# Moving one rounding step of a weight quantization from VectorE to ScalarE, and two small loads to the head of a queue

## What is computed

```python
def _L0_attn_ref(x, w_qkv, w_proj):
    qkv = (x @ w_qkv.T).reshape(B, N, 3, H, hd)
    att = softmax(einsum('bnid,bnjd->bnij', q, k) * scale)
    out = einsum('bnij,bnjd->bnid', att, v)
    return out.transpose(0, 2, 1, 3).reshape(B, N, D) @ w_proj.T
def fake_quant(x, bits, axes):
    qmax = 2.0 ** (bits - 1) - 1.0
    amax = jnp.max(jnp.abs(x), axis=axes, keepdims=True)
    scale = jnp.where(amax > 0, amax / qmax, jnp.ones_like(amax))
    return jnp.clip(jnp.round(x / scale), -qmax, qmax) * scale
def _L0_ffn_ref(x, kernel, bias):
    y = relu(fake_quant(x) @ fake_quant(kernel, 8, 0) + fake_quant(bias))
    return fake_quant(y)
x = x + _L0_attn_ref(_layernorm(x), w_qkv, w_proj)
x = x + _L0_ffn_ref(_layernorm(x), kernel, bias)
```

## Time and profile before

| what | value |
|---|---|
| median of 2 timed runs | 986.57 us (985.31 to 987.83) |
| the profiled execution's own time | 912.17 us |
| span of the slowest core (6) in it; the 8 cores | 910.6 us; 896.6 to 910.6 us |
| busy: PE, DVE, ACT, POOL | 690.0 (76%), 566.2 (62%), 323.1 (35%), 110.9 (12%) us |
| mean granted TensorE clock | 0.864 to 0.870 of full |

### The profile page before, as it was taken

One profiled execution on the slowest core, in us unless ns is written; L12 is line 12 of the kernel. 1 busy time (PEld: TensorE's weight loads), 2 busy tenths in 40 slices (PEclk: granted clock), 3 DMA queues, 4 the chain that ended last, 5 costly groups with the idle time before them and its releaser, 6 DMA issues.

```text
span 910.6 us, 10967 instructions; the slowest of 8 cores (896.6 to 910.6 us)
## 1 busy us (share of the span) xinstructions
PE 690.0 (76%) x3524; PEld 340.9 (37%) x3584; DVE 566.2 (62%) x949; ACT 323.1 (35%) x363; POOL 110.9 (12%) x93
## 2 busy tenths in 40 slices
PE   1147999899999999995565669954976647978790
PEld 1023444344444444443444434520433323434340
DVE  3353335535554554435777738981688895999996
ACT  3366334324333433434555521210221324433320
POOL 1001111112111211100000000012000000123214
PEclk9998999999999999996555569985897967989996
DMA  9552989989999999846532264379322200111112
GB/s 159 140 169 39 83 81 145 149 121 151 157 148 152 158 150 105 79 47 200 135 44 39 36 190 125 116 145 177 86 67 80 93 0 1 47 47 47 74 65 92
DMA packets 116984, 94.20 MB, mean 103 GB/s; under 512 B 101184, under 2 KB 101312, under 8 KB 113856
## 3 DMA queue, kind: packets, MB, share of 16 engines
q0 software_dynamic: 103680, 33.56, 38.0%
q1 hardware_dynamic: 13248, 59.94, 19.2%
HBM read 118.65 MB, written 8.39 MB: 140 GB/s over the span
## 4 chain that ended last, share of the span: by engine, by line
DVE 27%; issue 10%; PE 7%; DMA 6%; ACT 3%; DVEq 1%; POOLq 0%; POOL 0%; ACTq 0%; SPq 0%
DMA wpb<-wpT 4%; DMA ktb<-wkT 2%; DVE bnbuf L591 2%; DVE cols L656 2%; DVE ktb L688 2%; DVE kti L692 2%; DVE ttile L799 2%; DVE xr L557 2%; PE pF L538 2%; DVE cols L802 2%; ACT Ebuf L358 1%; DVE cols L389 1%; DVE Abuf L398 1%; ACT aTTbuf L366 1%; PE pF L344 1%
## 5 line engine op out<-in xcount | busy, mean ns | idle before, releaser
L289 PE MATMUL pF<-aT,wqb 128*128 128x512 bf16 x736 | 280.0, 380 | 1.6
L287 PE MATMUL pF<-aT,wqb 128*128 128x512 bf16 x706 | 268.5, 380 | 4.4 <-ACT qT L114 3.0
L538 PE MATMUL pF<-qk,xqs 128*128 128x512 bf16 x500 | 117.1, 394 | 4.6 <-ACT xqs L885 3.7
L502 PE MATMUL pF<-wpb,sT 128*128 128x512 bf16 x240 | 99.4, 414 | 24.7 <-DMA wpb<-wpT 23.1
L505 PE MATMUL pF<-wpb,sT 128*128 128x512 bf16 x256 | 106.2, 415 | 4.0 <-DMA wpb<-wpT 1.8
L287 PEld LDWEIGHTS pF<-aT,wqb 128*128 128x128 bf16 x736 | 72.2, 98 | 92.9 <-issue 6.9
L289 PEld LDWEIGHTS pF<-aT,wqb 128*128 128x128 bf16 x736 | 72.2, 98 | 87.1 <-issue 1.1
L302 POOL DMA_DIRECT2D wqb<-wqkvT x48 | 55.1, 1148 | 338.5 <-PE pF L289 248.3
L113 DVE CAST qT<-pF 128x512 bf16<-128x512 f32 x16 | 42.9, 2682 | 70.3 <-PE pF L289 55.9
L113 DVE CAST vT<-pF 128x512 bf16<-128x512 f32 x16 | 42.6, 2662 | 58.8 <-PE pF L289 58.8
L538 PEld LDWEIGHTS pF<-qk,xqs 128*128 128x128 bf16 x512 | 51.6, 101 | 67.5 <-issue 12.9
(11 more groups left out here) (116 smaller groups left out, 843.7 us busy)
## 6 DMA issues: line engine op xcount, KB each, us to landing
wqb<-wqkvT POOLq DMA_DIRECT2D x48, 512.0 KB, 10.4
ktc<-wkT SPq DMA_DIRECT2D x32, 512.0 KB, 8.6
ktb<-wkT SPq DMA_DIRECT2D x32, 512.0 KB, 4.0
xbuf<-x_att SPq DMA_DIRECT2D x8, 1024.0 KB, 6.8
xr<-x_res SPq DMA_DIRECT2D x8, 1024.0 KB, 7.5
wpb<-wpT POOLq DMA_DIRECT2D x32, 256.0 KB, 6.2
out<-xr SPq DMA_DIRECT2D x7, 1024.0 KB, 3.8
bias_b<-bias SPq DMA_DIRECT2D x1, 1024.0 KB, 4.6
```

What stands on the lines that cost most here:

```text
L287: tn.matmul(pa[:, :], wch, aT[:, 1024 * c:1024 * c + 512], start=st, stop=sp)
L289: mm = tn.matmul(pb[:, :], wch, aT[:, 1024 * c + 512:1024 * c + 1024], start=st, stop=sp)
L502: tn.matmul(pF[2 * (idx % 2)][:, :], lhs, wpb[:, 1024 * m:1024 * m + 512], start=st, stop=sp)
L538: mm = tn.matmul(pF[u][:, :], xqs[Mt % 2][:, 128 * c:128 * (c + 1)], qk[:, 2048 * c + 512 * u:2048 * c + 512 * (u + 1)], start=(c == 0), s ...
```

## The change

The subtraction of MAGIC (before L692, VectorE) becomes an activation on ScalarE (Identity with a bias column that holds -MAGIC, written once by a memset), in front of the copies of the same step. Two semaphores are used in a new way: `fKb` (VectorE has multiplied and added) and `fKv` (now: ScalarE has subtracted). `_sLnexp` moves two steps later. The loads of `ident` and the mask move in front of those of x.

```diff
@@ stage 1, SyncE
+            inc(sync.dma_start(ident[:, :], d_ident[:, :]), "aCn", 16)
+            inc(sync.dma_start(mask4[:, :], d_mask[:, :]), "aCn", 16)
             for t in range(NT):
-                if t == 2:
-                    inc(sync.dma_start(ident[:, :], d_ident[:, :]), "aCn", 16)
-                    inc(sync.dma_start(mask4[:, :], d_mask[:, :]), "aCn", 16)
                 if t >= 2:
@@ projection, VectorE
+            inc(v.memset(col(12), -MAGIC), "gNM")
             for i in range(2 * NC):
@@
-                h_qb = inc(v.tensor_scalar(ktb[i % 2][:, :], ktb[i % 2][:, :],
-                                           cols[:, 64 + ft:65 + ft], MAGIC,
-                                           ALU.mult, ALU.add), "selfV")
-                wt(v, h_qb)
-                h_kv = inc(v.tensor_scalar(kti[i % 2][:, :], ktb[i % 2][:, :],
-                                           MAGIC, None, ALU.subtract), "fKv")
+                inc(v.tensor_scalar(ktb[i % 2][:, :], ktb[i % 2][:, :],
+                                    cols[:, 64 + ft:65 + ft], MAGIC,
+                                    ALU.mult, ALU.add), "fKb")
                 if i >= 3:
                     v.wait_ge(S_("fFt"), 2 * i - 4)
-                wt(v, h_kv)
+                v.wait_ge(S_("fKv"), i + 1)
                 inc(v.tensor_scalar_mul(kqb[i % 3][:, :], kti[i % 2][:, :],
                                         cols[:, 48 + ft:49 + ft]), "fKg")
@@ projection, ScalarE
+            s.wait_ge(S_("gNM"), 1)
             for fidx in range(2 * NC):
                 ft, hh = fidx // 2, fidx % 2
+                s.wait_ge(S_("fKb"), fidx + 1)
+                if fidx >= 2:
+                    s.wait_ge(S_("fKg"), fidx - 1)
+                inc(s.activation(kti[fidx % 2][:, :], ktb[fidx % 2][:, :],
+                                 AF.Identity, bias=col(12)), "fKv")
                 for b2 in range(2):
@@
-                if fidx % 2 == 0 and 18 <= fidx <= 28:
-                    _sLnexp(s, (fidx - 18) // 2)
+                if fidx % 2 == 0 and 20 <= fidx <= 30:
+                    _sLnexp(s, (fidx - 20) // 2)
```

## The result

| | before | changed |
|---|---|---|
| median | 912.02 us (10 runs) | 970.12 us (11 runs) |
| ratio to before | | 1.0654, 95% interval 1.0633 to 1.0676 |
| the profiled execution's own time | 912.17 us | 968.65 us |
| spans of the 8 cores | 896.6 to 910.6 us | 953.6 to 967.1 us |

The change costs 6.5%. Four of the ten executions before (984.11 to 987.83 us) and four of the eleven after (996.45 to 1047.85 us) are slow ones, with a lower granted clock on some cores wherever the cores are on record; the medians contain them, the ratio leaves them out, and both executions behind the 986.57 us that stood before the prediction are among them.

What follows compares the result with a forecast made beforehand. In the projection stage PE was taken to bound the first half and DVE the second. Stage terms summing to 61.4 us, with 0.8 for the loads, made 62, added to the 986.57 us median: 1049 us, range 1022 to 1075.

Steps and rivals of the forecast that it cites:

- Rival 3: Projection stage: timed runs already wait there for ktb loads, the 74.4 us, leaving +8 us, 995 us; chance 6%.
- (a): Start of the projection stage: slower first subtraction, table load and first odd-step wait, +3.1 us.
- (b): First half, steps 2 to 14: six pairs at 13.29 us each, 79.7 against 47.7, +32.0 us.
- (c): Between the halves, steps 14 to 16: the wait for w_proj's second half moves along whole, 0 us.
- (d): Second half, steps 16 to 22: pairs of 13.29, 14.71 and 15.11 us, 43.1 against 25.5, +17.6 us.
- (e): Second half, steps 22 to 30: four pairs at 15.11 us plus 2.1 for _u2(0), +6.9 us.
- (f): Last pair, step 30's transposes to step 31's: 4.1 us against 2.31, +1.8 us.
- The price of the relay: Each pair, even step's transposes to odd step's: copies, subtraction, multiplication and hand-off take 3.7 us, PE standing 3.1.
- The clock: PE's matmul groups after the new gaps start at the lower clock, taking 8.5 us in place of 6.9.
- rival 1: PE's clock doesn't come back, every group at the lower level: +60 us, 1109 us; chance 6%.
- rival 2: PE's clock doesn't fall, all groups take 6.9 us: 1038 us, inside the range; chance 15%.
- Rival 4: Only DVE's relief counts, 1.6 us in each of seven DVE-bound pairs: 976 us; chance 2%.

Runs made afterwards that it cites:

- e4: Changed kernel with 44 needless transposes on PE between the even and odd steps' transposes of each pair: 956.57 us, ratio 1.0556 to the kernel before.
- e8: Kernel before, with the ktb loads for step 18 and later held back until group 8 is done: 913.4 us beside 911.73, one comparable execution.
- e9: Kernel before with subtraction and scaling fused on VectorE, and ktb loads from step 18 held until group 8 is done: ratio 0.9848 to before.
- e3: Kernel before with only the loads of ident and mask moved ahead of those of x: 907.16 us against 905.45, ratio 0.9998.
- e7: Changed kernel with a needless one-column activation ahead of ScalarE's first subtraction, so the table loads early: 966.22 us, taken once.
- e5: Kernel before with subtraction and scaling fused into one VectorE instruction, nothing moved to ScalarE: 891.19 us against 904.70, ratio 0.9857.
- e2: Changed kernel with ScalarE subtracting step i+1 before it copies step i: 921.75 us, ratio 1.0178 to the kernel before.
- e6: Changed kernel, ScalarE subtracting one step ahead into bfloat16 kqb, VectorE's first multiplication also ahead, ident and mask loads back: 900.28 us against 904.70, ratio 0.9949.

## Why the prediction was right in its mechanism, and wrong in its time

The direction, the mechanism and the size of the step were right: 62 us and +6.3% forecast, 58.1 us between the medians (60.2 between those of the executions that the ratio keeps) and 6.5% by the ratio measured; on the profiled execution 974 forecast, 968.65 measured. The time wasn't: 1049 us forecast, with 1022 at the low end, and 970.12 measured. **The step that failed is the last of the total: "I add the 62 to the median".** The row at hand said 912.17, the median of two said 986.57, and the text itself noted that no row said where the 74.4 us lay. They weren't in the kernel: ten executions have a median of 912.02. Adding to the profile's own time would have given 974 and a range around it that holds the result; 1022 to 1075 doesn't. Rival 3 was built on the same 74.4 us and falls with it. That the 62 came as near as 56.5 is in part luck, since the misses in the terms below have both signs.

Term by term, on the two profiled executions (core 6 before, core 2 after):

| term | forecast | measured |
|---|---|---|
| first multiplication of the stage, 538.91 before, 540.71 after | 0.8 for the two loads | +1.8 |
| (a) from there to T(2) | +3.1 | +2.5 |
| (b) T(2) to T(14), 47.7 us before | +32.0 | +30.5 |
| (c) T(14) to T(16), 41.55 before | 0 | -6.1 |
| (d) T(16) to T(22), 25.5 before | +17.6 | +18.8 |
| (e) T(22) to T(30), 55.6 before | +6.9 | +8.2 |
| (f) T(30) to T(31), 2.31 before | +1.8 | +1.8 |
| from there to the end | 0 | -1.1 |
| sum | 62 | 56.5 |

(The 538.91 is the first L688 of the stage before.) The two columns are of different cores. By the medians of the eight cores (b) is +30.7, (c) -4.4, (d) +18.6, (e) +8.2 and (f) +1.8, so the table isn't an accident of the cores chosen.

- **The price of the relay**, 3.7 us: 3.71 measured. ScalarE's subtraction was taken at 1.1 and is 1.15, its two bounds 0.69 and 2.10. With 1.15 the four parts make 3.70, so the hand-off to DVE and the overlap on ACT cancel out.
- **The Trainium skill's estimate for the subtraction.** By the Trainium skill, page "ScalarE: Activation LUTs", section "What ACT_TABLE_LOAD costs", the estimate was 1.13 us. Measured in the changed kernel are 1.147 to 1.161 us, median 1.148, so this trace agrees; the 1.1 that I took was 4% too low.
- **The clock**: seen as forecast, 13.1 to 13.4 us in five of the six pairs from T(2) to T(14) against 13.29, and 11.7 in the sixth. e4 prices it: 8.0 us in (b) and about 9 in all; I had 1.6 us in each of seven pairs, 11. Neither rival 1 nor rival 2 came about: five pairs lie between them, and the one of 11.7 is what rival 2 would have had in all.
- **(c)** was the largest miss of a term, put at 0 because the stall was taken to move along whole. It shrank by 6.1 us on these cores and 4.4 by the medians. VectorE, stopped at step 17, freed fewer buffers, so that three loads of ktb landed beside w_proj in place of five; e8 and e9 show that fewer loads shorten it.
- **(d) and (e)** are 1.2 and 1.3 us above. In (d) it is the first pair, 14.7 us in place of 13.29: T(16) to T(17) is 3.96, group 9 begins 1.51 behind T(17) and takes 9.3. In (e) it is _part2: its nine small instructions stand on VectorE between the multiplications of steps 24 and 25, and of 26 and 27, and there T to T is 4.89 and 4.71 us where the forecast has 4.1. I had left them out.
- **The two loads**: mis-sized at 0.8; e3 has 0 within 2 us. The +1.8 ahead of the stage most likely isn't theirs: e3's QKV matmuls don't start later by the median of the cores, and the stage's first multiplication differs more from core to core in one execution, 528.4 to 540.7 us before and 527.0 to 540.7 in the changed kernel. Its cause stays open.
- **The table load** counted in full (e7).
- **Rival 4**, the relief of VectorE, was rightly excluded for this order. e5 shows what it was worth, 1.4%, once it cost no wait.
- **The signs named**: T(14) is at 635.88 (near 636), and 3.10 us of waiting for kqb stand at each odd T from T(3) to T(15). PE's waits for kqb are 68.0 us (some 60), and the stage ends at 784 us (near 788), by (c). T(2p) to T(2p+1) is near 3.7 only up to pair 9; from T(20) on it is 4.1 to 6.1, as terms (d) and (e) had it and the list of signs didn't.

## What to carry to other kernels

Before moving an instruction to a less busy engine, write down what stands in front of it in that engine's order and follow each wait back: here a copy that waits for transposes that wait for a whole group of matmuls. That order cost 5 of the 6.5%; the slower engine, the hand-offs and the table load cost 1.5, and the same subtraction one step earlier in the order gives 4.8 back. The engine that a profile names as the releaser is worth a look too: in e2 it named copies that had long been done. An engine at 35% busy isn't free if its next instruction is always waiting, and here the saving on the busy engine was to be had by fusing two of its operations, which adds no wait at all (1.4% faster). When timed runs and the profiled execution disagree by far more than runs of one kernel do, the forecast is a difference: give it as a ratio to the profiled time, and treat the gap as a question about the runs.

## What the hardware showed that I had not expected

- Gaps of 3.1 us and 0.5 us, with 0.6 us of transposes in between, stood alike ahead of groups 2 to 7 of the changed kernel. In five of these six groups TensorE went to the lower level at or near the start (matmuls of 0.58 to 0.63 us, 1.2 GHz), and the granted clock was 0.84 from 563 to 571 us, in group 2; in group 6 it didn't (1.00 from 616 to 622.5 us). With 2.6 us of needless transposes in the gap it stayed at 1.00 from 564 to 610 us (e4).
- VectorE scales 128x1024 bfloat16 into bfloat16 in 0.48 us (e6), where int32 or float32 into bfloat16 take 0.75.
- Three 512 KB loads of ktb taken out of a stretch in which 16 loads of w_proj ran made it 3.0 us (e9 against e5) and 4.5 us (e8) shorter by the medians of the cores, and the kernel no faster.
